# Splitting the second and third batch like the later ones in a graph layer, with reordered loads

## The reference, cut to what matters

```python
h = jnp.maximum(_layernorm(x, axis=-1), 0.0)
HW  = einsum('bnf,rfo->rbno', h, W[:, :F]) + einsum('rd,rdo->ro', W_edges, W[:, F:])[:, None, None, :]
AHW = einsum('rbnm,rbmo->rbno', A, HW)          # A: adj, adj, shift, adj^T, adj^T, shift^T, eye
x = x + max(AHW, axis=0) + b
```

## Time and profile before

| | |
|---|---|
| median of 3 runs | 205.33 us (205.29 to 205.62) |
| the profiled execution, its own time | 205.48 us |
| its span, first to last instruction | 203.7 us |
| PE busy | 197.7 us, 97% |
| DVE, ACT, POOL busy | 170.0, 160.1, 115.8 us |

### The profile page before, as it was taken

How to read it: one execution, slowest core, us unless ns; L and a number is a source line. 1 busy time by engine, 2 the same in 40 slices (tenths; PEclk the granted TensorE clock), 3 DMA queues, 4 the chain that set the end, 5 groups by cost and what they waited for, 6 DMA issues and landing times.

```text
span 203.7 us, 3448 instructions
## 1 busy us (share of the span) xinstructions
PE 197.7 (97%) x918; PEld 151.2 (74%) x918; DVE 170.0 (83%) x411; ACT 160.1 (79%) x432; POOL 115.8 (57%) x162
## 2 busy tenths in 40 slices
PE   6999999999999999999999999999999999999991
PEld 6456466778787787878778787878878787887871
DVE  3487969989898998989989898998989899878565
ACT  3887989996969879696988969697896969795230
POOL 4041341477574938657592956759295675939500
PEclk9999999999999999999999999999999999999999
DMA  5999999997888979789987969799795969570501
GB/s 161 333 356 358 373 346 273 293 357 191 258 315 232 350 183 342 201 269 306 292 304 162 381 153 333 228 246 357 198 395 107 312 199 343 208 154 0 100 4 51
DMA packets 33748, 51.07 MB, mean 251 GB/s; under 512 B 1873, under 2 KB 11329, under 8 KB 33729
## 3 DMA queue, kind: packets, MB, share of 16 engines
q1 hardware_dynamic: 31152, 46.53, 67.1%
q0 software_dynamic: 2304, 4.20, 13.3%
q10 hardware_dynamic: 272, 0.13, 0.2%
HBM read 46.65 MB, written 4.19 MB: 250 GB/s over the span
## 4 chain that ended last, share of the span: by engine, by line
PE 94%; DMA 2%; DVE 2%; SPq 0%; issue 0%; DVEq 0%
PE bank_p L870 13%; PE bank_p L871 11%; PE bank_p L872 10%; PE bank_g L832 6%; PE bank_g L835 6%; PE bank_g L841 6%; PE bank_gT L818 6%; PE bank_gT L812 6%; PE bank_gT L808 6%; PE bank_p L741 3%; PE bank_p L860 3%; PE bank_p L749 3%; DMA adj_sb<-in_adj_dram 2%; PE bank_g L789 2%; PE bank_gT L780 2%; PE bank_g L770 2%
## 5 line engine op out<-in xcount | busy, mean ns | idle before, releaser
L334 POOL TENSOR_TENSOR a_lo<-adj_sb,a_hi 128x512 fp32r<-128x512 f32 x26 | 33.1, 1296 | 31.6 <-DVE a_lo L596 28.5
L640 DVE TENSOR_TENSOR best<-bank_p,best 128x512 f32<-128x512 f32 x48 | 33.1, 691 | 7.2 <-PE bank_p L872 6.0
L422 ACT ACTIVATE a_hi<-adj_sb 128x512 fp32r<-128x512 f32 x56 | 34.5, 620 | 1.3 <-DMA adj_sb<-in_adj_dram 1.3
L431 ACT ACTIVATE aT_hi<-adjT_sb 128x512 fp32r<-128x512 f32 x56 | 34.4, 620 | 0.0
L341 POOL TENSOR_TENSOR aT_lo<-adjT_sb,aT_hi 128x512 fp32r<-128x512 f32 x26 | 33.2, 1297 | 0.9 <-ACT aT_hi L431 0.3
L327 POOL TENSOR_TENSOR o_sb<-best,x_bias 128x512 f32<-128x512 f32 x15 | 19.8, 1317 | 19.1 <-DVE aT_lo L603 15.9
L637 DVE SCALAR_TENSOR_TENSOR best<-bank_p,c_col,best 128x512 f32<-128x512 f32 x32 | 24.0, 750 | 6.6 <-ACT best L480 6.0
L461 ACT ACTIVATE gT_hi<-bank_gT 128x512 fp32r<-128x512 f32 x16 | 9.5, 595 | 25.0 <-PE bank_gT L818 24.7
L443 ACT ACTIVATE h<-x_sb,shift,rstd 128x128 f32<-128x128 f32 x60 | 24.7, 488 | 0.0
L870 PE MATMUL bank_p<-hT_hi,w_hi 128*128 128x512 f32 x48 | 20.0, 417 | 0.0
L872 PE MATMUL bank_p<-hT_lo,w_hi 128*128 128x512 f32 x48 | 18.7, 390 | 0.0
(11 more groups left out here) (122 smaller groups left out, 477.7 us busy)
## 6 DMA issues: line engine op xcount, KB each, us to landing
adj_sb<-in_adj_dram SPq DMA_DIRECT2D x15, 1024.0 KB, 7.5
adjT_sb<-in_adjT_dram SPq DMA_DIRECT2D x15, 1024.0 KB, 8.3
x_bias<-in_biasT_dram SPq DMA_DIRECT2D x16, 256.0 KB, 6.5
x_bias<-in_xT_dram POOLq DMA_DIRECT2D x16, 256.0 KB, 4.1
x_sb<-in_x_dram SPq DMA_DIRECT2D x15, 256.0 KB, 8.3
out_dram<-o_sb SPq DMA_DIRECT2D x15, 256.0 KB, 5.5
adj_sb<-in_adj_dram SPq DMA_DIRECT2D x4, 256.0 KB, 5.1
adjT_sb<-in_adjT_dram SPq DMA_DIRECT2D x4, 256.0 KB, 5.1
```

Of the source, the lines that this page charges most:

```text
L334: nc.gpsimd.tensor_tensor(a_lo[q][:, c, :], adj_sb[q][:, c, :], a_hi[q][:, c, :].bitcast(F32), ALU.subtract).then_inc(alo_last_ready, 1)
L422: nc.scalar.activation(a_hi[q][:, c, :], adj_sb[q][:, c, :], ACT.Copy, accum_out=sums[q][:, 0, c:c + 1]).then_inc(ahi_ready, 1)
L431: nc.scalar.activation(aT_hi[q][:, c, :], adjT_sb[q][:, c, :], ACT.Copy, accum_out=sums[q][:, 1, c:c + 1]).then_inc(aThi_ready, 1)
L640: op = nc.vector.tensor_tensor(best[q][:, :], product, best[q][:, :], ALU.max)
```

## The change

`FIRST` becomes 1: batches 1 and 2 make both aggregates in three fast passes over all four chunks, as the later batches do. The float32 variants go. With it come splits of batch 1 on ACT, DVE and POOL, and of the rest of batch 2. The lists of ACT, DVE and POOL are written out anew up to batch 3; behind that they keep their steps in nearly the same order. Product 6 of batch 0 goes to `bank_p0` in place of `bank_g` (after `begin_best(0)` has read product 0 there), so that `aggregate(1)` needs not wait for batch 0's maxima. Loads of `adj` and `adjT` from batch 3 on wait for the splits of the batch two before (POOL's too), no longer for its aggregates on PE; `adjT` is issued ahead of the store, and the stores of batches 0 and 1 move behind the loads of batch 4.

Its core (left out: the same replacement in `aggregate` as in `aggregate_T`, the names `first_bank_of` and `summed`, and the removed float32 functions):

```diff
-FIRST = 2
+FIRST = 1
...
             def load_adj(b):
...
                 if b >= 2 + FIRST:
                     sp.wait_ge(ahi_ready, (b - 1 - FIRST) * NS)
                     sp.wait_ge(alo_ready, (b - 1 - FIRST) * ND)
-                if b > 2 + FIRST:
-                    sp.wait_ge(alo_last_ready, (b - 2 - FIRST) * NG)
+                    sp.wait_ge(alo_last_ready, (b - 1 - FIRST) * NG)
...
             load_bias(0)
+            load_bias(1)
+            load_adj(2)
             load_x(3)
-            load_adj(2)
             load_adjT(2)
-            load_bias(1)
             for b in range(1, B):
                 if b + 3 < B:
                     load_x(b + 3)
                 if b + 2 < B:
                     load_adj(b + 2)
-                store(b - 1)
-                if b + 1 < B:
-                    load_bias(b + 1)
-                if b + 2 < B:
                     load_adjT(b + 2)
+                if b == 1:
+                    continue
+                for done in range(0 if b == 2 else b - 1, b):
+                    store(done)
+                    if done + 2 < B:
+                        load_bias(done + 2)
...  POOL
+            pool.wait_ge(alo_ready, ND)
+            pool.wait_ge(hlo_ready, 1)
+            split_adj_last(1)
+            part_sums(1)
+            pool.wait_ge(aTlo_ready, ND)
+            split_adjT_last(1)
             add_bias(0)
-            part_sums(1)
-            finish(0)
             add_bias(1)
+            pool.wait_ge(alo_ready, 2 * ND)
+            split_adj_last(2)
+            split_adjT_last(2)
             part_sums(2)
-            add_bias(2)
             for b in range(2, B):
                 pool.wait_ge(aTlo_ready, (b - FIRST + 1) * ND)
+                if b == 2:
+                    finish(0)
                 finish(b - 1)
+                if b == 2:
+                    add_bias(2)
                 if b + 1 < B:
                     pool.wait_ge(alo_ready, (b - FIRST + 2) * ND)
                     pool.wait_ge(hlo_ready, b - FIRST + 2)
                     split_adj_last(b + 1)
...  ACT, after make_h(1)
-            copy_sumsT(0)
             act.wait_ge(ccol_ready, 1)
             begin_best(0)
-            sum_adj(1)
+            split_adj(1, range(HALF))
+            copy_sumsT(0)
+            split_adj(1, range(HALF, C))
+            split_adjT(1)
+            split_gT(1)
+            split_hT(1)
+            split_adj(2)
+            split_g(1)
+            copy_sumsT(1)
+            begin_best(1)
             std_of(2)
+            make_h(2)
+            split_adjT(2)
+            split_gT(2)
+            split_hT(2)
+            split_adj(3)
+            split_g(2)
+            copy_sumsT(2)
+            begin_best(2)
+            std_of(3)
+            make_h(3)
+            split_adjT(3)
+            std_of(4)
+            for b in range(3, B):
+                if b < B - 1:
                     split_adj(b + 1)
                 split_gT(b)
                 split_hT(b)
-                if 2 <= b < B - 2:
-                    std_of(b + 2)
                 if b + 1 < B:
                     make_h(b + 1)
                 split_g(b)
                 copy_sumsT(b)
                 begin_best(b)
...
+                if b + 2 < B:
                     std_of(b + 2)
                 if b + 1 < B:
                     split_adjT(b + 1)
...  DVE, after split_g_lo(0)
+            take_best(0, 1, 0)
+            split_adj_lo(1)
+            split_h_lo(1)
+            take_best(0, 2, 1)
+            take_best(0, 6, 2)
+            take_best(0, 3, 3)
+            split_adjT_lo(1)
+            split_hT_lo(1)
+            split_gT_lo(1)
+            take_best(0, 4, 4)
+            take_best(0, 5, 5)
             variance(2)
+            split_g_lo(1)
+            scale_and_shift(2)
+            split_adj_lo(2)
+            take_best(1, 1, 0)
+            take_best(1, 2, 1)
+            split_h_lo(2)
             for i in range(NH, NPROD):
+                take_best(1, i, i - 1)
+            split_adjT_lo(2)
+            split_gT_lo(2)
+            split_hT_lo(2)
             variance(3)
+            split_g_lo(2)
             scale_and_shift(3)
+            split_adj_lo(3)
+            take_best(2, 1, 0)
+            take_best(2, 2, 1)
+            split_h_lo(3)
             for i in range(NH, NPROD):
+                take_best(2, i, i - 1)
+            variance(4)
+            scale_and_shift(4)
+            for b in range(3, B):
+                split_adjT_lo(b)
+                if 3 < b < B - 2:
                     variance(b + 2)
                 split_gT_lo(b)
                 split_hT_lo(b)
+                if b == 3:
+                    variance(b + 2)
                 if b + 1 < B:
                     split_adj_lo(b + 1)
                     split_h_lo(b + 1)
                 split_g_lo(b)
                 for i in range(1, NPROD - int(b == B - 1)):
-                    take_best(b, i)
+                    take_best(b, i, i - 1)
+                if b + 2 < B:
+                    scale_and_shift(b + 2)
...  PE
             def aggregate_T(b):
...
-                if b == FIRST:
-                    pe.wait_ge(adj_in[q], times(b))
-                    for c in range(ND, C):
-                        nc.tensor.matmul(bank_gT[:, 0:N], h[q][:, c, :], adj_sb[q][:, c, :],
-                                         start=(c == ND), stop=False)
-                for c in split_chunks(b):
+                for c in range(C):
                     pe.wait_ge(ahi_ready, (b - FIRST) * NS + c + 1)
...
             def aggregate(b):
                 q = b % 2
-                pe.wait_ge(best_done, b * NBEST)
+                if b > FIRST:
+                    pe.wait_ge(best_done, b * NBEST)
...
                 product(0, 2)
-                passes(6, bank_of[6][:, 0:N], start=True)
+                pe.wait_ge(best_begun, 1)
+                passes(6, first_bank_of[6][:, 0:N], start=True)
```

More of the change, by code:

```diff
@@ L396, in std_of, with split_adj @@
                                      bias=eps[:, :]).then_inc(std_ready, 1)
-            def sum_adj(b):
-                q = b % 2
-                act.wait_ge(adj_in[q], times(b))
-                for c in range(C):
-                    last = nc.scalar.activation(summed[q][:, 0, c, :], adj_sb[q][:, c, :], ACT.Copy,
-                                                accum_out=sums[q][:, 0, c:c + 1])
-                last.then_inc(sums_ready, 1)
-            def sum_adjT(b):
-                q = b % 2
-                act.wait_ge(adjT_in[q], times(b))
-                for c in range(C):
-                    last = nc.scalar.activation(summed[q][:, 1, c, :], adjT_sb[q][:, c, :], ACT.Copy,
-                                                accum_out=sums[q][:, 1, c:c + 1])
-                last.then_inc(sums_ready, 1)
-            def split_adj(b):
+            def split_adj(b, chunks=range(C)):
                 q = b % 2
@@ L419, in split_adj @@
                     act.wait_ge(gT_psum, b - 1)
-                act.wait_ge(parts_lo, b - 1)
-                for c in range(C):
+                if b >= 2:
+                    act.wait_ge(parts_lo, b - 1)
+                for c in chunks:
                     nc.scalar.activation(a_hi[q][:, c, :], adj_sb[q][:, c, :], ACT.Copy,
@@ L504, in _ @@
                 act.wait_ge(adj0_in[c], 16)
-                last = nc.scalar.activation(summed[0][:, 0, c, :], adj_sb[0][:, c, :], ACT.Copy,
+                last = nc.scalar.activation(summed[:, 0, c, :], adj_sb[0][:, c, :], ACT.Copy,
                                             accum_out=sums[0][:, 0, c:c + 1])
@@ L511, in _ @@
                 act.wait_ge(adjT0_in[c], 16)
-                last = nc.scalar.activation(summed[0][:, 1, c, :], adjT_sb[0][:, c, :], ACT.Copy,
+                last = nc.scalar.activation(summed[:, 1, c, :], adjT_sb[0][:, c, :], ACT.Copy,
                                             accum_out=sums[0][:, 1, c:c + 1])
@@ L517, in _ @@
             make_h(1)
-            copy_sumsT(0)
             act.wait_ge(ccol_ready, 1)
             begin_best(0)
-            sum_adj(1)
-            std_of(2)
-            sum_adjT(1)
-            for b in range(1, B):
-                if 2 <= b < B - 1:
+            split_adj(1, range(HALF))
[8 more added lines that the diff above has]
+            begin_best(1)
+            std_of(2)
+            make_h(2)
[12 more added lines that the diff above has]
+                if b < B - 1:
                     split_adj(b + 1)
@@ L536, in _ @@
                 begin_best(b)
-                if b == 1:
-                    split_adj(b + 1)
+                if b + 2 < B:
                     std_of(b + 2)
@@ L918, in _ @@
             for b in range(1, B):
-                if b < FIRST:
-                    aggregate_T_whole(b)
-                else:
-                    aggregate_T(b)
+                aggregate_T(b)
                 turn_h(b)
-                if b < FIRST:
```

(4 more changed lines are left out.)

91 lines of the change are left out of this document (23 added, 68 removed).

## The result

The changed kernel takes 210.04 us, the median of 4 runs (209.77 to 210.92); the kernel before took 205.48 in the 4 runs beside it (205.29 to 205.80). The ratio is 1.0227, 95% interval 1.0208 to 1.0246. The change costs 4.56 us. The forecast was a loss of 2.8, 208.1, and its range ended at 209.4: the sign and the late root on ACT came as forecast, the size did not, and the time lies outside the range.

A forecast was written before the change was run, and what follows sets the result against it. PE was taken as the bound, busy 194.82 of 195.00 us. The sum 205.48 - 2.47 (PE's saving) + 1.4 (batch 0) + 0.2 (batch 1) + 3.7 (batch 3) = 208.3, 208.1 against the median; range 205.9 to 209.4.

The forecast's parts named there:

- the late root on ACT: Batch 3: ACT's std_of(4) waits for DVE's variance(4) until 49.1, so split_gT(3) starts at 51.8, PE's result being there since 48.0.
- PE's saving in batch 2: Two chunks in three fast passes instead of float32 save PE 0.70 us; the batch then takes 11.80.
- the wait in batch 0: PE's product (0, 2) waits 1.4 us for copy_sumsT(0), which ACT reaches only after four other things.
- Batch 2, no wait found: Batch 2: every operand is ready over half a microsecond before PE, so PE does not wait.
- The loss in batch 3: PE waits some 3.7 us in all in batch 3; begin_products(3) starts at 57.4 against 54.60 before, 2.8 later.
- the first rival: PE stays the bound: variance(4) comes early enough that ACT meets gT(3) on time, giving 204.4, faster; chance 0.13.
- POOL's rival: Batch 3: POOL, not ACT, is late, add_bias(2) waiting for a late bias load ahead of split_adj_last(3); 205.3; chance 0.06.
- The clock: Rival: gaps on PE lower its clock; one aggregate at 1.2 GHz would add 2.8, so 210.9; chance 0.02.
- Bounds: Whole time: 206.7 without the wait in batch 0; 209.3 if a dozen hops were each 0.1 longer.

The follow-up runs named there:

- POOL cut: The changed kernel with POOL's 12 subtractions for the low parts of batches 1 to 3 cut to 64 of 512 columns: 209.04 us, ratio 1.0161.
- experiment 7: The changed kernel with variance(4) on DVE ahead of the four later maxima of batch 2: 209.86 us, ratio 1.0211.
- experiment 4: The changed kernel with add_bias(2) behind split_adj_last(3) on POOL instead of ahead of it: 211.05 us, ratio 1.0274.
- experiment 14: The changed kernel with finish(0) between POOL's two pairs of subtractions of batch 2, store(0) and load_bias(2) moved to follow it: 210.30 us, ratio 1.0230.
- the probe: The kernel before with six DVE instructions behind its last maximum, each alone, then beside two POOL subtractions 128x512; the 128x4 product went from 0.16 to 1.21 us.
- experiment 3: The changed kernel with POOL starting split_adj_last(2) only when DVE has made h_lo of batch 2: 210.27 us, ratio 1.0249.
- experiment 12: The changed kernel with adj and adjT loads from batch 3 on waiting for PE's aggregates again, adjT behind the store from batch 5: 211.86 us, ratio 1.0296.
- experiment 1: The changed kernel with batch 4's root behind split_hT(3) on ACT and scale_and_shift(4) behind split_hT_lo(3) on DVE: 213.08 us, ratio 1.0376.
- experiment 13: The changed kernel with adj and adjT loads waiting for PE's aggregates again, adjT behind the store, only from batch 7 on: 210.56 us, ratio 1.0260.

## Why the prediction was wrong

**PE's saving in batch 2 and the wait in batch 0 came as forecast.** Batch 0 grew by 1.32 (forecast 1.4, PE's wait 1.05 by the profile), and with POOL cut batch 2 fell to 11.78 (11.80). The new bank for product 6 showed no wait.

**The step that failed is "Batch 2, no wait found", and with it the durations of DVE.** Every DVE duration was taken from the earlier trace rows, measured where POOL happens to be idle or DVE reads PSUM. POOL got eight more subtractions (x30 in place of x26 for `adj`, the same for `adjT`), those of batch 3 came later than before, and I asked only whether they fit into POOL's own time. They hold DVE's instructions with SBUF operands. In the table, batch 2 was off by 0.85, batch 3 by 0.71 (4.41 in place of 3.7), batch 1 by 0.39. The first goes when POOL is cut, and the second nearly so (15.64). The one of batch 1 stays in every column and is another error, 0.25 of it in one hop: product (1, 0) came 6.85 into the batch, against 27.9 - 21.3 = 6.6 by the forecast, because ACT had the transposed `h` split only 4.15 into it, not 25.1 - 21.3 = 3.8, and DVE's last maxima of batch 0 stand behind that. With POOL cut the kernel is close to the one that the forecast described: 3.13 against 2.8. The trace of before had shown it, in batch 0. DVE's timeline there, and POOL's:

```profile
13.80 0.72 DVE L589 SCALAR_TENSOR_TENSOR shift<-mean_var,rstd 128x4 f32<-128x4 f32 x1
```
```profile
13.76 0.74 POOL L364 TENSOR_TENSOR w_lo<-w_sb,w_hi 128x256 fp32r<-128x256 f32 x1 [2.59 <-DVE w_hi L673]
```

Beside a subtraction of POOL's the shift of batch 1 took 0.72 in place of 0.16. I had not looked there.

**The loss in batch 3 was put to the right instruction, but to one gate where there are two.** ACT idled 2.45 before the root, and `gT_hi(3)` came at 53.53 (forecast 51.8). From the start of the batch that is 6.66, against 51.8 - 45.3 = 6.5, so ACT's part was sized right. From there to begin_products(3), at 59.79 (forecast 57.4), it was 6.26 in place of 5.6: DVE, held by POOL until 53.36, came to `gT` 0.39 after ACT had split it, and two low parts for batch 4 beside `finish` took 1.55 in place of 1.28. Nor would an early root have freed DVE: in experiment 7 the shift still ended with POOL's last subtraction, 6.01 into the batch in place of 6.49. This was the first rival, "`variance(4)` comes early enough", with 204.4: ACT met `gT(3)` on time, and the time was 209.86. Its price assumed that nothing stood behind the first gate. Of the 1.87 by which the forecast missed the table's sum (4.70 - 2.83), the 0.85 of batch 2 and the 0.66 here are thus DVE held by POOL.

**POOL's rival** was closer than its 0.06: the bias came on POOL at 47.46, and its a_lo kept PE waiting for 0.40 and 0.72. Taking these waits away (experiments 4 and 14) gave nothing back, but both edits moved other work, so what they cost alone is not shown; the path by which POOL mattered, the hold, was not in this rival.

**The clock** stayed at 1.00 up to the end of PE's work in the changed kernel's profile. It fell in some experiments (below).

**Bounds.** The upper one let each hop be 0.1 longer; an instruction that goes from 0.16 to 1.95 is not such an error, so the range was too narrow on that side.

## What to carry to other kernels

Before giving work to an idle engine, look at what its neighbour does at that moment: on this chip a subtraction on GpSimd and a DVE instruction with two SBUF operands run one after the other, and a small DVE instruction can wait for the whole of a large one (0.16 became 1.21 us in the probe). Read durations by where they stand, not by their mean; a 128x4 product that takes 0.72 in one place and 0.16 in another is a sign to follow. When one wait is removed and the time stays, there may be two gates: only the run with both removed tells what they are worth together, and whether a third stands behind them.

## What the runs showed of the hardware

- The hold acts both ways (POOL's 1.26 became 1.71 in the probe) and also on a copy with one SBUF operand (0.41 to 1.47), not on an operand in PSUM, bn_stats or a small reciprocal.
- In the probe DVE got in between two subtractions of POOL's, and so it did at 36.75 in experiment 3. In the changed kernel the shift at 51.41 waited through the end of one and all of the next, and in experiment 12 the one at 51.49, with its 3.44 us, through parts or all of three. In the first two cases POOL's first subtraction took 1.26 and 1.27, and the next began 0.04 before its end. In the last two they stand right behind a DMA issue of POOL's, took 1.54 to 1.57 each, and still began 1.23 to 1.26 apart, so that each began 0.3 before the one ahead had ended. The issue goes with it: in experiment 4 the pair ahead of it took 1.30 each and the pair behind it 1.55, and in experiment 14, with no issue near, 1.28 to 1.30. That DVE can't get in because the subtractions overlap is a guess; no run tests it.
- The clock of PE fell behind a wait of 3.17 us (0.59 from 60 to 64 us in experiment 1), but in experiment 3 it was 0.57 in the same stretch, where PE was busy 2.68 of the 4 us before it, exactly as in the changed kernel and in experiment 13, which stayed at 1.00. The Trainium skill, TensorE: Matmul & The Clock Gate, Part 1: The HAM clock gate (the "warmup" mystery), says that an idle PE is throttled; that gaps like these can lower the clock agrees with it, but the same gaps gave both levels here.
